# Squares that take the row sum as bias, in a kernel of 32 samples with split float32 products

## The reference

```
h  = relu(x @ W1[l] + b1[l])               # 512 -> 128, l = language of the sample
y  = x + h @ W2[l] + b2[l]                 # 128 -> 512
n  = (y - mean(y)) * rsqrt(var(y) + 1e-5)  # over the 512 columns
x1 = x + n * gamma[l] + beta[l]
out = x1 + x1 @ W[c] + b[c]                # 512 -> 512, c = category of the sample
```

## Time and profile before

| | us |
|---|---|
| median of 3 runs | 611.79 |
| lowest and highest | 609.99, 613.36 |
| the profiled execution, whole | 614.65 |
| its span, first to last instruction | 612.8 |
| TensorE busy | 601.9 |
| GpSimd busy | 559.4 |
| VectorE busy | 525.1 |
| ScalarE busy | 522.1 |

### The profile page before, as it was taken

The page is one execution under the profiler, slowest core; times in us unless marked ns, Lnnn a source line. Parts: engine busy times, 40 slices in busy tenths (PEclk is TensorE's granted clock), DMA queues, the critical chain, the costliest instruction groups (busy, mean ns, idle before and its releaser), DMA issues.

```text
span 612.8 us, 10739 instructions
## 1 busy us (share of the span) xinstructions
PE 601.9 (98%) x2891; PEld 495.3 (81%) x2891; DVE 525.1 (86%) x1151; ACT 522.1 (85%) x770; POOL 559.4 (91%) x263
## 2 busy tenths in 40 slices
PE   9879999999999999999999999999999999999998
PEld 7657787888888888888888888888888888888887
DVE  1769988898998899999889899889899889899673
ACT  4867889998888989888989888989889989888770
POOL 5757899999999999999999999999999999999830
PEclk9998999999999999999999999999999999999999
DMA  9999999999999999999999999999999999997222
GB/s 297 282 271 230 267 290 275 325 298 283 302 274 274 322 300 260 303 279 299 281 295 252 306 282 293 280 312 264 295 277 286 287 312 269 296 290 266 86 87 103
DMA packets 125939, 166.23 MB, mean 271 GB/s; under 512 B 11062, under 2 KB 72768, under 8 KB 121812
## 3 DMA queue, kind: packets, MB, share of 16 engines
q1 hardware_dynamic: 125524, 165.32, 96.2%
q10 hardware_dynamic: 288, 0.52, 0.3%
q0 software_dynamic: 96, 0.05, 0.0%
HBM read 132.17 MB, written 33.55 MB: 270 GB/s over the span
## 4 chain that ended last, share of the span: by engine, by line
PE 86%; DMA 4%; SPq 4%; DVE 2%; issue 2%; ACT 2%; DVEq 0%; ACTq 0%
PE o_bank L830 18%; PE o_bank L832 18%; PE o_bank L831 17%; PE n_bank L848 8%; PE d_bank L832 6%; PE d_bank L830 6%; PE d_bank L831 6%; PE y_bank L830 2%; PE y_bank L832 2%; PE y_bank L831 2%; DMA out<-out_half 2%; SPq L251 2%; DMA x_quad<-in_x 1%; DMA w_raw<-in_L_cond_W 1%; ACT x_tok L550 1%
## 5 line engine op out<-in xcount | busy, mean ns | idle before, releaser
L830 PE MATMUL o_bank<-w_hi,x1T_hi 128*128 128x512 f32 x512 | 205.7, 402 | 1.2 <-DVE x1T_lo L723 1.2
L832 PE MATMUL o_bank<-w_hi,x1T_lo 128*128 128x512 f32 x512 | 200.2, 391 | 0.0
L831 PE MATMUL o_bank<-w_lo,x1T_hi 128*128 128x512 f32 x512 | 199.2, 389 | 0.0
L441 POOL TENSOR_TENSOR w_lo<-w_raw,w_hi 128x1024 fp32r<-128x1024 f32 x62 | 147.8, 2408 | 10.2 <-ACT w_hi L524 10.2
L514 ACT ACTIVATE norm<-y,neg_mean_rstd,rstd 128x512 f32<-128x512 f32 x128 | 153.0, 1271 | 1.1 <-DVE neg_mean_rstd L708 1.1
L436 POOL TENSOR_TENSOR x_tok<-x_tok,b_bc 128x1024 f32<-128x1024 f32 x60 | 143.9, 2422 | 10.0 <-DMA b_bc<-in_L_cond_b 9.8
L407 POOL TENSOR_TENSOR xs_lo<-xT,xs_hi 128x2048 fp32r<-128x2048 f32 x28 | 129.5, 4624 | 1.4 <-ACT xs_hi L566 0.5
L658 DVE STREAM_TRANSPOSE xT<-x_quad 128x512 f32<-128x512 f32 x120 | 126.9, 1099 | 3.1 <-DMA x_quad<-in_x 3.1
L550 ACT ACTIVATE x_tok<-y,neg_mean 128x512 f32<-128x512 f32 x128 | 91.5, 717 | 33.6 <-DVE neg_mean L678 33.6
L830 PEld LDWEIGHTS o_bank<-w_hi,x1T_hi 128*128 128x128 f32 x512 | 96.3, 188 | 22.9 <-issue 2.8
L735 DVE TENSOR_TENSOR out_half<-o_bank,b_bc 128x512 f32<-128x512 f32 x127 | 86.9, 685 | 32.3 <-PE o_bank L832 30.8
(11 more groups left out here) (93 smaller groups left out, 825.1 us busy)
## 6 DMA issues: line engine op xcount, KB each, us to landing
w_raw<-in_L_cond_W SPq DMA_DIRECT2D x32, 1024.0 KB, 7.3
out<-out_half SPq DMA_DIRECT2D x63, 512.0 KB, 7.8
x_tok<-in_x SPq DMA_DIRECT2D x31, 1024.0 KB, 9.5
x_quad<-in_x SPq DMA_DIRECT2D x120, 256.0 KB, 8.3
w_raw<-in_L_cond_W SPq DMA_DIRECT2D x64, 256.0 KB, 4.0
b_bc<-in_L_cond_b SPq DMA_DIRECT2D x64, 256.0 KB, 7.5
x_tok<-in_x ACTq DMA_DIRECT2D x2, 256.0 KB, 3.4
x_tok<-in_x SPq DMA_DIRECT2D x2, 256.0 KB, 4.1
```

The costliest lines, as they stand in the source:

```text
L441: pool.tensor_tensor(w_lo[q][:, c:c + 2, :], w_raw[q][:, c:c + 2, :], w_hi[q][:, c:c + 2, :].bitcast(F32), ALU.subtract).then_inc(w_lo_don ...
L830: pe.matmul(acc, lhs_hi, rhs_hi, start=first, stop=False)
L831: pe.matmul(acc, lhs_hi, rhs_lo, start=False, stop=False)
L832: return pe.matmul(acc, lhs_lo, rhs_hi, start=False, stop=last)
```

## The change

The square becomes the square of (sum - 512 y), which is 512^2 (y - mean)^2: the row sum itself is the bias and -512 the scale. The sum of squares is then larger by 512^2, and the two places that divide it by 512 divide by 512^3. `mean`, its buffer and its semaphore are dropped. ScalarE's square waits for y_done alone. VectorE's `variance`, which reads `y_sum`, waits for the last y itself, since no mean stands in front of it any more. Where the squares stand in ScalarE's order is unchanged.

```
--- before.py
+++ after.py
@@ -117,7 +117,6 @@
         y = sb("y", [P, NT, H])
 
         y_sum = sb("y_sum", [P, NT])
-        neg_mean = sb("neg_mean", [P, NT])
         sq_sum = sb("sq_sum", [P, NT])
         std = sb("std", [P, NT])
         r0 = sb("r0", [P, NT])
@@ -218,7 +217,6 @@
         x1_lo_done = sem("x1_lo_done")
         h_lo_done = sem("h_lo_done")
         y_done = sem("y_done")
-        mean_done = sem("mean_done")
         stat_done = sem("stat_done")
         rstd_only_done = sem("rstd_only_done")
         rstd_done = sem("rstd_done")
@@ -546,13 +544,12 @@
             def square(k, t):
 
                 act.wait_ge(y_done, k.count(NT, 0, t + 1))
-                act.wait_ge(mean_done, k.count(NT, 0, t + 1))
-                act.activation(x_tok[k.b][:, t, :], y[:, t, :], ACT.Square, bias=neg_mean[:, t:t + 1],
+                act.activation(x_tok[k.b][:, t, :], y[:, t, :], ACT.Square, scale=-float(H), bias=y_sum[:, t:t + 1],
                                accum_out=sq_sum[:, t:t + 1]).then_inc(sq_done, 1)
 
             def deviation(k):
                 act.wait_ge(sq_done, k.count(NT, 0, NT))
-                act.activation(std[:, :], sq_sum[:, :], ACT.Sqrt, scale=1.0 / H,
+                act.activation(std[:, :], sq_sum[:, :], ACT.Sqrt, scale=1.0 / H ** 3,
                                bias=eps[:, 0:1]).then_inc(std_done, 1)
 
             def high_w1_of_next(k):
@@ -673,24 +670,18 @@
                                          ALU.mult, ALU.add, accum_out=y_sum[:, t:t + 1]
                                          ).then_inc(y_done, 1)
 
-            def mean(k, t):
-                dve.wait_ge(y_done, k.count(NT, 0, t + 1))
-                dve.tensor_scalar(neg_mean[:, t:t + 1], y_sum[:, t:t + 1], -1.0 / H, None, ALU.mult
-                                  ).then_inc(mean_done, 1)
-
             def y_pair(k, i):
 
                 if i == 0 and k.since(2):
                     dve.wait_ge(norm_done, k.count(NT, 0, 0))
                 y_tile(k, 2 * i)
                 y_tile(k, 2 * i + 1)
-                mean(k, 2 * i)
-                mean(k, 2 * i + 1)
 
             def variance(k):
+                dve.wait_ge(y_done, k.count(NT, 0, NT))
                 dve.tensor_scalar(neg_mean_copy, y_sum[:, :], -1.0 / H, None, ALU.mult).then_inc(stat_done, 1)
                 dve.wait_ge(sq_done, k.count(NT, 0, NT))
-                dve.tensor_scalar(var_eps, sq_sum[:, :], 1.0 / H, EPS, ALU.mult, ALU.add).then_inc(stat_done, 1)
+                dve.tensor_scalar(var_eps, sq_sum[:, :], 1.0 / H ** 3, EPS, ALU.mult, ALU.add).then_inc(stat_done, 1)
 
             def inverse_deviation(k):
 
@@ -784,7 +775,6 @@
             low_h(k0)
             for t in range(NT):
                 y_tile(k0, t)
-                mean(k0, t)
             variance(k0)
             inverse_deviation(k0)
             turn_next_x(k1, 0)
```

More of the change, by code:

```diff
@@ L674, in y_tile @@
                                          ).then_inc(y_done, 1)
[L676 to L679, removed]
             def y_pair(k, i):
```

## The result

| | before | after |
|---|---|---|
| median of 9 runs, us | 611.79 | 617.53 |
| lowest to highest | 609.99 to 613.36 | 614.85 to 621.02 |
| span of the profiled execution | 612.8 | 618.7 |

The ratio is 1.0094, with a 95% interval of 1.0071 to 1.0117. I had forecast 609.6 with a range to 612.2, and gave slower 0.05.

A forecast was written before the change was run, and what follows sets the result against it. TensorE was taken as the bound, at a clean pace of 18.21 us a sample. Gains of 1.34 at the early waits and 0.81 in later small losses, 2.15 in all, took 611.79 to 609.6 us, range 607.6 to 612.2.

The forecast's parts named there:

- (1): VectorE loses four instructions a sample; both means of a pair take 0.27 us together in a steady sample.
- My slower rival: Earlier x load delays the w2 load, ScalarE stalls and ReLU is late: 614.8 us, chance 0.04.
- The chain: Row sums through squares and reciprocal to x1T_lo, which TensorE awaits: 0.74 us earlier in a steady sample.
- (2): ScalarE's first square needs only the first y's sum: starts 0.75 us earlier, the last ends 0.83 earlier.
- (3): VectorE's fourth y and x1 operations limit the reciprocal to 0.74 us earlier, not 0.83.
- (4): Price of ScalarE's new square with fixed scale and bias from memory: 0 over the old 0.72 us.
- (5): VectorE's wait for the last y in the variance is over when reached: nil.
- (6): SP's 1 MB x load, waiting 20.9 us for squares in 23 waits, starts up to 0.8 us earlier.
- The crumbs: Small TensorE losses over 26 samples from 108.16 us, 18.241 each against 18.21: 0.81 us to win back.
- The start: TensorE's x1T_lo waits at 56.57 and 94.80 us shrink: 1.34 us gained by 95 us (0.74 to 1.68).

The follow-up runs named there:

- means ahead: Changed kernel with the means kept, unread, only in the eight samples ahead of VectorE's loop; ratio 0.9973.
- the unused buffer: Changed kernel with 24 more waiting instructions at VectorE's start and neg_mean still set aside, unused; ratio 0.998.
- 200 waits: Kernel before with 200 more instructions at VectorE's start that only wait for a flag long set; ratio 1.0313.
- the unrolled kernel: Changed kernel with VectorE's loop written out so it never jumps back, other engines keeping theirs; ratio 0.9992.

## Why the prediction was wrong

**The step that failed** is (1): "VectorE loses four instructions a sample". I counted their time and nothing else; for their places in the stream the sum had no term, that is, nil. What decided was these places: 32 instructions fewer ahead of the loop moved its start from 340 to 308, across the edge at 332 (the 24 fewer in the loop alone do no harm, as the run with means ahead shows), and two jumps back that had cost nothing visible then cost 4.85 and 5.57 us on VectorE. TensorE paid 6.15 us of these: 20.15 + 22.20 + 18.48 less three samples of 18.226. Nothing in the views of before shows how near the loop stood to an edge; the compiled stream gives the loop's place, and only the runs gave the edge. My slower rival named transfers of w2 that come late; ScalarE waited for them once, 1.9 us, so the side was right there by another cause.

**The chain, (2) and (3): right.** One steady sample after, on VectorE, ScalarE and TensorE:

```profile
309.49 0.08 DVE L669 DVE_READ_ACCUMULATOR y<-d_bank,x_tok 128x1 f32 x1
...
309.61 0.72 ACT L547 ACTIVATE x_tok<-y,y_sum 128x512 f32<-128x512 f32 x1
...
310.73 0.71 PE L838 MATMUL n_bank<-ident,norm 128*128 128x128 f32 x5
...
313.00 0.17 DVE L690 RECIPROCAL r<-std 128x4 f32<-128x4 f32 x1
...
313.99 1.40 DVE L714 SCALAR_TENSOR_TENSOR x1T_lo<-n_bank,params,x1T_hi 128x512 fp32r<-128x512 f32 x2
```

The mark of the sample in the earlier trace rows, before:

```profile
308.87 1.03 PE L848 MATMUL n_bank<-ident,norm 128*128 128x128 f32 x8
```

The square starts 0.04 us behind the first y's sum. The reciprocal starts 2.27 behind the mark; before it was 3.09 (311.96 in the earlier trace rows). That is 0.82 earlier, where I had 0.74. The low part of x1 starts 3.26 behind the mark, before 3.98 (312.85): 0.72 earlier.

**The price, (4): nil, right.** The squares' group on the page has 713 ns each after:

```profile
L547 ACT ACTIVATE x_tok<-y,y_sum 128x512 f32<-128x512 f32 x128 | 91.1, 713 | 13.5 <-DVE y L669 10.7
```

**The wait in the variance, (5): nil, right**, by the run with means ahead, whose loop has it. **The x load, (6): right.** SP's wait for the squares fell from 20.9 us to

```profile
SPq L254 <- ACT x_tok L547: 0.9, 3, 0.6
```

and in the kernels without stops no harm from it can be seen.

**The crumbs: right in kind, half in size.** They are gone: outside the stops the marks stand evenly. But in the changed kernel they stand 18.226 apart, not 18.21, so of 0.81 us only 0.39 came back (474.27 less 26 x 18.226). With the unused buffer the even spacing is 18.213 and 0.72 came back.

**The start: open.** I had 1.34 us for it. My signs for it, no wait for x1T_lo at 56 and under 0.5 us at 94, did not come: the changed kernel still lost 2.1 us to x1T_lo, in two waits, the second one sample earlier than before. A store on that chain took 12.55 us, not less than before:

```profile
56.41 0.47 PE L820 MATMUL o_bank<-w_hi,x1T_hi 128*128 128x512 f32 x1 [1.09 <-DVE x1T_lo L714]
...
76.60 0.47 PE L820 MATMUL o_bank<-w_hi,x1T_hi 128*128 128x512 f32 x1 [1.03 <-DVE x1T_lo L714]
```

```profile
57.55 12.55 DMA out<-out_half
```

But the marks near 108 scatter by themselves: 108.16 and 105.83 in the kernel before, 108.32 and 104.16 in the changed one, 103.57 to 106.70 in the other nine that have the new squares at the start and no 200 waits ahead. The means, 105.3 of eleven with the new squares and 107.0 of two without, lean the forecast way, but one profile each can't tell 1.34 us in this scatter. Nor can the times: the five kernels with the new squares and no stops that were run several times have ratios of 0.9973, 0.998, 0.999, 0.9992 and 0.9997, a gain of 0.2 to 1.7 us. Less the 0.4 of the crumbs without the buffer or the 0.7 with it, between -0.2 and 1.0 us is left for the start, inside the intervals.

So the chain that I described is there, and its gain is small, as a forecast of "within 0.5%" says; how much of the 2.2 us it gives is shown only for the crumbs. It was outweighed by 6.15 us from a cost that I did not look for.

## What to carry to other kernels

An instruction taken out of a hand-written loop is a change of place as well as of work. When a change moves the time by something that its own chain can't explain, look for stops at the jump back of a loop, one per iteration, with instruction packets in the transfers and "issue" as releaser (in 8 of the 14 stops here; the other 6 were put down to TensorE), and test with instructions that do nothing: pushing the loop by a few dozen places is a cheap experiment and sometimes the repair. Compare two versions of a kernel only after each has been seen free of such stops.

## What the runs showed of the hardware

- VectorE's jump back stopped it for 4.1 to 6.5 us in every kernel whose loop starts at 308 to 324 or at 540, and did nothing visible in those whose loop starts at 332 or 340. Blocks of 128 instructions, four of them touched by the loops that stop and three by the others, give all of it and fit the packets; blocks of 256 give the same outcomes. Where the target lies eight instructions ahead of an edge, there were two stops in a row, 6.50 and 4.63 us.
- Every profile with such stops has 30 instruction packets on queue 14, or 33 with the 200 waits; every profile without them has 20 or 21, and the unrolled kernel 23. The packets are of 8 KB. For this kernel the count tells the two kinds apart at a glance.
- 200 instructions that only wait, ahead of VectorE's first work, made that work start at 21.37 us instead of 8.66 and 9.20.
- 16 bytes of address: with `neg_mean` set aside, used or not, TensorE's even spacing is 18.213 us a sample, without it 18.226 (473.55 against 473.90 over 26 samples for the same stream of instructions, one profile each; the other kernels with the new squares and no stops agree, 473.54 against 473.89 twice). All buffers behind it lie 16 bytes elsewhere. Which of them matters was not tried.
